# A gated expert FFN on one Trainium2 core: the last batch's second tile is weighted on ScalarE and added on GpSimd

## The reference

```python
def _gated_ffn(x, wi0, wi1, wo):
    return gelu(x @ wi0) * (x @ wi1) @ wo          # 512 -> 2048 -> 512
share_out  = _gated_ffn(x, sWi0, sWi1, sWo)
expert_out = _gated_ffn(x, Wi0[label], Wi1[label], Wo[label])
gate_in = concatenate([expert_out[:, 0], share_out[:, 0]], axis=-1)   # first row of each
weights = softmax(relu(gate_in @ g0) @ g1)
return x + expert_out * weights[:, 0] + share_out * weights[:, 1]
```

## Time and profile before

| | us |
|---|---|
| median of 3 runs (lowest, highest) | 1970.09 (1969.66, 1970.26) |
| time of the profiled execution | 1969.45 |
| its span, first to last instruction | 1967.7 |
| around the span | 1.75 |
| TensorE busy | 1960.2 |
| VectorE busy | 1525.7 |
| ScalarE busy | 1037.6 |
| GpSimd busy | 76.8 |
| granted TensorE clock, mean | 0.999 |

### The profile page before, as it was taken

The page is one execution under the profiler, slowest core; times in us unless marked ns, Lnnn a source line. Parts: engine busy times, 40 slices in busy tenths (PEclk is TensorE's granted clock), DMA queues, the critical chain, the costliest instruction groups (busy, mean ns, idle before and its releaser), DMA issues.

```text
span 1967.7 us, 29050 instructions
## 1 busy us (share of the span) xinstructions
PE 1960.2 (100%) x11168; PEld 1729.5 (88%) x11168; DVE 1525.7 (78%) x1823; ACT 1037.6 (53%) x1376; POOL 76.8 (4%) x56
## 2 busy tenths in 40 slices
PE   9999999999999999999999999999999999999998
PEld 8988888899998888889999888889999988888997
DVE  8776667789888676778988767668898976766887
ACT  6564444466666444446666644344666664444564
POOL 0000000001000000000101000000010100000000
PEclk9999999999999999999999999999999999999999
DMA  5431111244452111124445311112444421111242
GB/s 161 142 105 54 59 49 54 65 154 146 141 182 85 60 53 49 54 86 140 157 146 164 97 49 54 52 56 81 154 148 145 161 91 49 54 59 49 90 158 108
DMA packets 152429, 194.83 MB, mean 99 GB/s; under 512 B 10467, under 2 KB 116963, under 8 KB 150499
## 3 DMA queue, kind: packets, MB, share of 16 engines
q1 hardware_dynamic: 152290, 192.98, 31.0%
HBM read 184.55 MB, written 8.39 MB: 98 GB/s over the span
## 4 chain that ended last, share of the span: by engine, by line
PE 98%; DVE 1%; issue 0%; ACT 0%; DMA 0%; SPq 0%; POOL 0%; DVEq 0%; POOLq 0%; ACTq 0%
PE ps_outs L424 35%; PE ps_pv L405 18%; PE ps_pv L415 18%; PE ps_c L405 14%; PE ps_c L415 13%; DMA x_src<-x_cols 0%; DVE xl L868 0%; DVE s_out L1231 0%; DVE x_src L919 0%; DVE a_src L887 0%; DVE al L868 0%; POOL gate_row L1258 0%; ACT ah L645 0%; ACT ah L627 0%; ACT wo0h L657 0%
## 5 line engine op out<-in xcount | busy, mean ns | idle before, releaser
L868 DVE TENSOR_TENSOR al<-a_src,ah 128x1024 fp32r<-128x1024 f32 (+3 forms) x291 | 400.9, 1379 | 34.5 <-ACT ah L627 33.4
L627 ACT CAST ah<-a_src 128x1024 fp32r<-128x1024 f32 (+2 forms) x284 | 334.8, 1190 | 1.7 <-DVE a_src L887 1.2
L405 PE MATMUL ps_pv<-xh,al 128*128 128x256 f32 x1008 | 285.3, 283 | 0.4 <-ACT ps_pv L752 0.4
L405 PE MATMUL ps_pv<-xl,ah 128*128 128x256 f32 x1008 | 285.3, 283 | 0.0
L405 PE MATMUL ps_pv<-xh,ah 128*128 128x256 f32 x1008 | 285.3, 283 | 0.0
L677 ACT ACTIVATE act<-ps_c 128x256 f32<-128x256 f32 (+1 forms) x192 | 87.5, 456 | 309.4 <-PE ps_c L405 172.2
L743 ACT COPY ps_pv<-ps_c 128x512 f32<-128x512 f32 x127 | 72.5, 571 | 268.4 <-PE ps_c L415 182.1
L405 PE MATMUL ps_c<-xh,ah 128*128 128x256 f32 x756 | 213.9, 283 | 0.0
L405 PE MATMUL ps_c<-xl,ah 128*128 128x256 f32 x756 | 213.9, 283 | 0.0
L405 PE MATMUL ps_c<-xh,al 128*128 128x256 f32 x756 | 213.6, 283 | 0.0
L424 PE MATMUL ps_outs<-wo0h,hidl 128*128 128x512 f32 x512 | 199.6, 390 | 0.0
(11 more groups left out here) (119 smaller groups left out, 3942.4 us busy)
## 6 DMA issues: line engine op xcount, KB each, us to landing
a_src<-experts SPq DMA_DIRECT2D x255, 256.0 KB, 3.8
raw_wo<-experts SPq DMA_DIRECT2D x128, 256.0 KB, 2.8
a_src<-shared SPq DMA_DIRECT2D x128, 256.0 KB, 3.0
g_sb<-g_rows SPq DMA_DIRECT2D x16, 1024.0 KB, 5.4
raw_wo<-shared SPq DMA_DIRECT2D x64, 256.0 KB, 2.8
x_src<-x_cols SPq DMA_DIRECT2D x32, 256.0 KB, 4.0
g_sb<-x_rows SPq DMA_DIRECT2D x7, 1024.0 KB, 4.9
out<-s_out SPq DMA_DIRECT2D x7, 1024.0 KB, 6.9
```

Source lines behind the costliest of these rows:

```text
L405: mm = nc.tensor.matmul(ps[:, a * HALF:(a + 1) * HALF], a_op[ap][:, i, a, k, :], x_op[xp][:, j, k, h, :], start=(start and a == 0 and k == ...
L627: nc.scalar.copy(a_op[HI][:, i:j, :, :, :], a_src[m % 2][:, i:j, :, :, :]).then_inc(a_hi_done, 1)
L868: nc.vector.tensor_tensor(to, of, hi.bitcast(F32), ALU.subtract).then_inc(done, 1)
```

## The change

The second tile (m = 1) is taken from VectorE. ScalarE multiplies its PSUM bank by the weight into `act[:, GATE, 0, :]`, a buffer in SBUF that is free by then, and GpSimd adds the input rows to it with a `tensor_tensor` of 128x512 elements. VectorE makes tiles 0, 2 and 3. The stores are issued in the order 0, 2, 1, 3, the third of them waiting for GpSimd.

```diff
+        second_weighted = sem("second_weighted")
+        second_mixed = sem("second_mixed")
@@ block.sync
-            for m in range(MC):
-                sp.wait_ge(last_mixed, m + 1)
+            for m, done, count in ((0, last_mixed, 1), (2, last_mixed, 2), (1, second_mixed, 1), (3, last_mixed, 3)):
+                sp.wait_ge(done, count)
                 sp.dma_start(out[BATCH - 1, :, m, :], s_out[:, 1, m, :]).then_inc(out_stored, 16)
@@ block.scalar, behind exponentials(BATCH - 1)
+            sc.wait_ge(last_down_done, 2)
+            sc.wait_ge(weight_step, BATCH * 2)
+            nc.scalar.activation(act[:, GATE, 0, :], ps_out[1], ACT.Copy, scale=gate_w[:, EXPERT:EXPERT + 1]
+                                 ).then_inc(second_weighted, 1)
@@ block.vector
-            for m in range(MC):
+            for m in (0, 2, 3):
                 dve.wait_ge(last_down_done, m + 1)
@@ block.gpsimd, behind sum_logits(BATCH - 1)
+            pool.wait_ge(second_weighted, 1)
+            pool.wait_ge(rows_added, 2)
+            nc.gpsimd.tensor_tensor(s_out[:, 1, 1, :], act[:, GATE, 0, :], last_rows[0][:, 1, :], ALU.add
+                                    ).then_inc(second_mixed, 1)
```

## The result

| | before | after |
|---|---|---|
| median of 13 runs each (lowest, highest), us | 1969.87 (1969.51, 1970.30) | 1974.80 (1974.28, 1976.22) |
| time of the profiled execution, us | 1969.45 | 1974.34 |
| its span, us | 1967.7 | 1972.6 |

The ratio after to before is 1.0025, with a 95% interval of 1.0017 to 1.0032: 4.9 us slower. That is a little over the 0.2% that I called the limit of what can be told, though the interval's lower end lies under it. The forecast was 1973.7 us in a range of 1969.6 to 1976.6.

The account below looks back on a forecast made before the run. TensorE bounds the kernel, so only the tail could move. A 5.8 us GpSimd load from 1961.06, the 1.30 us addition and two late stores gave +3.6 us on 1970.09: 1973.7 us, range 1969.6 to 1976.6.

Parts of the forecast that it names:

- Where the ground lies: Tail behind the matmuls: the change can touch only the 5.3 us between the weight and the end.
- VectorE's operation worth nothing: Tiles on VectorE: one operation fewer saves 0.66 us of pace, but DMA pace sets the end; gain taken as 0.
- ScalarE's operation: Tile 1 from PSUM on ScalarE: 0.60 us, starting at 1962.44 behind the weight at 1962.34, covered while GpSimd is later.
- GpSimd's addition: Addition for tile 1 on GpSimd: 1.30 us, the short end of 28 differences of the same shape.
- Where the pair stands: MODIFY_POOL_CONFIG pair on GpSimd: runs at 1961.06, 0.36 us behind the all-reduce's start, not held by the wait for ScalarE.
- rival D: GpSimd's pair stands behind the wait for ScalarE's tile, load starts at 1963.1: +5.6 us, 1975.7 us; chance 0.07.
- The price of the load: GpSimd's code load between all-reduce and addition: 5.8 us, taken from the loads toward the broadcast.
- rival B: GpSimd's load toward the addition is longer, slower by over 0.2% from 6.15 us; at 7.3 us, 1975.2 us; chance 0.33.
- The rest of the sum: Last two stores: DMA data 0.85 us behind the issue, two stores of 0.70 us, then 0.9 us to the span's end.
- within 0.2%: Whole kernel's time: no change beyond 0.2%, or 3.9 us; chance 0.55, against 0.42 for slower and 0.03 for faster.
- A: The forecast itself: GpSimd's load costs 5.6 to 6.1 us, time 1973.4 to 1974.0 us; chance 0.40.
- C: No GpSimd load worth naming toward the addition, which runs from 1963.1: 1970.0 us; chance 0.15.

Follow-up runs that it names:

- e6: Kernel after the change, with GpSimd's addition left out and tile 1 stored uncomputed right behind tile 2: 1970.29 us, ratio 1.0002 to the kernel before.
- e5: Kernel before the change, with the last batch's all-reduce left out (VectorE copies the unsummed logits): 1969.80 us, ratio 0.9999.
- e4: Kernel after the change, with the last batch's all-reduce left out (VectorE copies the unsummed logits): 1969.77 us, ratio 1.0000 to the kernel before.
- e2: Kernel after the change, with a small add and a small broadcast on GpSimd between the last all-reduce and the addition: 1988.81 us, ratio 1.0097.
- e3: Kernel after the change, with stores in the order 0, 2, 3, 1: 1974.17 us, ratio 1.0021 to the kernel before.
- e8: Kernel before the change, plus a 128x4 add on GpSimd behind the last all-reduce that only the program's end waits for: 1970.71 us, ratio 1.0004.
- e1: Kernel after the change, but VectorE instead of GpSimd adds the rows to ScalarE's tile: 1969.80 us, ratio 1.0000 to the kernel before.
- e7: Kernel before the change, with the first tile made and stored in two halves of 256 columns: 1970.04 us, ratio 1.0000.

## Why the prediction came out as it did

**Where the ground lies: right.** Only the tail moved. TensorE's part is the same but for the start's 0.45 us.

**VectorE's operation worth nothing: right**, and shown. e6 gives less than 0.1 us for it where 0.66 us of work went, and e5 against e4 gives none.

**ScalarE's operation: nearly right.** It took 0.69 us and not 0.60, started 0.10 us behind the weight as forecast, needed no table load, and was covered.

**GpSimd's addition: right.** 1.25 us against 1.30.

**Where the pair stands: right.** It ran 0.35 us behind the all-reduce's start, before `second_weighted` was met (rival D falls by this row alone).

**The price of the load: this is the step that failed.** "I take the price of the other direction, 5.8, because it is the same pair of instructions and the nearest row by far." It is the same pair, but the directions are not alike. Toward the additions the loads took 6.7 us (after), 6.7 and 6.9 (e2), 7.2 (e3) and 7.2 (e8); toward the broadcasts 5.7 in e2's tail and 5.6 to 6.0 in the loop, where each of the ten profiles shows three of them (the longest is in e1, from the pair at 955.4 to the broadcast at 961.40). The two groups don't overlap. The mechanism was right and this term too small by 0.9 us, which makes it rival B, past its point of 6.15 us. The rule of the Trainium skill, GPSIMD Engine Reference, Instruction dispatch (about 6 us, 5.95 measured, for the first call to freshly loaded code) has the mechanism, and it warned rightly against zero; its one figure lies at the upper end of the loads toward the broadcasts and is too low for the direction that counted.

**The rest of the sum: right.** From the third store's issue to the span's end it was 3.1 us, where the forecast's terms give 3.15 (0.85, twice 0.70, 0.9). So of the 4.9 us between the two profiles, 3.6 are the forecast's, 0.9 are the load's direction, 0.45 the start's scatter, and 0.05 goes off for the shorter addition. By the tail, which is free of the start, the change costs 4.45 us, or 0.23%. The medians of 13 runs differ by 4.9 us, and there one execution's start does not count. Whether their other 0.5 us is a later start in most runs of the kernel after, or a load that is mostly longer than the 6.7 us of its profile, as it was in e3 and e8, no trace shows.

The chances leaned to "within 0.2%" (0.55 against 0.42). That rested on the 5.8, which put the forecast 0.3 us under the limit; with a row for only one direction, it deserved less trust than that. Nor does the range say much for the 5.8: from 1969.6 to 1976.6 it held the points of A, B at 7.3, C and D alike. The rise itself was 4.9 us and not 3.6; the time came out 1.1 us off and not 1.3 only because the kernel before measured 1969.87 beside it and not 1970.09.

What stays open: why the load toward the additions scatters between 6.7 and 7.2 us. The stores in flight beside it don't order it (two stores 6.7, three 7.2, four 7.2, but none 6.9). Why this direction is dearer was not tested either; a larger piece of code would fit, and nothing here shows it.

## What to carry to other kernels

An operation moved to an idle engine brings with it whatever that engine must change to run it. On GpSimd, look at what ran there just before: between a broadcast or an all-reduce over partitions and a `tensor_tensor` it lost 5.6 to 7.2 us here behind a pair of MODIFY_POOL_CONFIG, and that is free only where the engine waits that long anyway. Before shortening a chain of small operations in front of stores, see whether the DMA engines have a hole between the stores: without one, faster work behind the first store moved nothing (e6), and an earlier first store gained nothing while the stores behind it came later (e7).

## What the runs showed of the hardware that I had not expected

- The load for a change of kind on GpSimd costs 6.7 to 7.2 us toward `tensor_tensor` (five times, all in the tail) and 5.6 to 6.0 us toward the broadcast, in the idle tail as in the busy loop, and even for 128x4 elements (0.19 us of work).
- ScalarE's copy of 128x512 out of PSUM with a scale read per partition took 687 ns, where the plain copy took 590 and the Copy with a constant scale, from SBUF into PSUM, 594.
- The first tile's store in two halves of 128 KB kept the DMA engines for 1.0 us, where the whole one took 0.78; the three whole tiles behind it took 2.2 us either way (e7).
